# Front of a two-layer graph kernel: products of W a on GpSimd, casts on ScalarE, LayerNorm's scales one step later

## The reference, cut to what matters

```python
h = relu(layernorm(x))
x = x + L0(h, adj, adj, ...)
h = relu(layernorm(x))
x = x + L1(h, adj, W_stack)

# L0
attn_a = sigmoid(concat([adj @ x, x]) @ Wa.T + ba)      # attn_b in the same way
h = x @ W_sa
scores = (h @ a_sa[0, :256])[:, None] + (h @ a_sa[0, 256:])[None, :]
e = where(adj != 0, exp(-leaky_relu(scores, 0.01)), 0)
x_a = (e / (sum(e) + 1e-5)) @ h
x_b = adj @ (x @ W_gcnb) + b_gcnb
return sigmoid(attn_a * x_a + attn_b * x_b)

# L1, twice
Wh, Ws = split(x @ W)
x = leaky_relu((softmax(Wh @ Ws.T) * adj) @ Wh + x)
```

## Time and profile before

| | |
|---|---|
| time, median of 3 runs | 1635.68 us (1634.53 to 1636.81) |
| profiled execution, its own time | 1637.55 us |
| its span in the profile | 1635.7 us |
| granted TensorE clock, mean | 0.994 |
| PE busy | 1566.5 us (96%) |
| DVE busy | 1173.8 us (72%) |
| ACT busy | 1071.0 us (65%) |
| POOL busy | 999.2 us (61%) |
| TensorE busy, first of 40 slices / second | 5 tenths / 9 tenths |

### The profile page before, as it was taken

How to read it: one execution, slowest core, us unless ns; L and a number is a source line. 1 busy time by engine, 2 the same in 40 slices (tenths; PEclk the granted TensorE clock), 3 DMA queues, 4 the chain that set the end, 5 groups by cost and what they waited for, 6 DMA issues and landing times.

```text
span 1635.7 us, 34736 instructions
## 1 busy us (share of the span) xinstructions
PE 1566.5 (96%) x12902; PEld 1541.2 (94%) x12902; DVE 1173.8 (72%) x2165; ACT 1071.0 (65%) x2090; POOL 999.2 (61%) x874
## 2 busy tenths in 40 slices
PE   5999999999999999999999999999999999999984
PEld 5999999999999999999999999999999999999984
DVE  6766766667665677777777778756777777777774
ACT  3579889899984566666666666646666666666653
POOL 2112222222210588888888888838888888888896
PEclk9999999999999999999999999999999999999998
DMA  4124444544430233333333335412333333333332
GB/s 145 40 59 117 123 117 117 146 120 117 123 85 27 55 97 96 98 98 97 98 97 98 98 97 187 156 40 85 102 98 97 99 102 98 98 98 98 98 105 70
DMA packets 88666, 163.36 MB, mean 100 GB/s; under 512 B 9265, under 2 KB 19376, under 8 KB 88240
## 3 DMA queue, kind: packets, MB, share of 16 engines
q1 hardware_dynamic: 60624, 113.41, 23.6%
q0 software_dynamic: 24336, 44.31, 11.0%
q10 hardware_dynamic: 3536, 3.41, 0.6%
HBM read 147.99 MB, written 13.11 MB: 98 GB/s over the span
## 4 chain that ended last, share of the span: by engine, by line
PE 73%; POOL 11%; issue 7%; DVE 4%; ACT 3%; DMA 0%; POOLq 0%; SPq 0%; DVEq 0%; ACTq 0%
PE PS L1128 25%; PE PS L1333 8%; PE PS L1336 7%; PE PS L1335 7%; POOL FR L431 5%; PE PS L1203 5%; PE PS L1200 5%; PE PS L1202 5%; PE PS L1199 5%; PE PS L1201 5%; POOL X L424 5%; DVE AF L953 1%; ACT FR L592 1%; ACT ROW L612 1%; POOL PAB L424 0%
## 5 line engine op out<-in xcount | busy, mean ns | idle before, releaser
L1128 PE MATMUL PS<-FR,RB 128*128 128x256 f32 x4056 | 540.1, 282 | 3.8 <-ACT X L574 1.8
L431 POOL TENSOR_TENSOR FR<-AF,FR 128x512 fp32r<-128x512 f32 x338 | 450.5, 1333 | 134.8 <-ACT FR L592 134.8
L1128 PEld LDWEIGHTS PS<-FR,RB 128*128 128x128 f32 x4056 | 500.7, 188 | 12.3 <-ACT X L574 10.7
L424 POOL TENSOR_TENSOR X<-X,ROW 128x512 f32<-128x512 f32 x294 | 398.9, 1357 | 82.2 <-ACT ROW L602 82.2
L1333 PE MATMUL PS<-FR,RA 128*128 128x256 f32 x1352 | 389.0, 288 | 26.2 <-POOL FR L431 26.1
L1336 PE MATMUL PS<-FR,RA 128*128 128x256 f32 x1352 | 379.7, 281 | 0.0
L1335 PE MATMUL PS<-FR,RA 128*128 128x256 f32 x1352 | 379.0, 280 | 0.0
L953 DVE TENSOR_TENSOR AF<-PS,AJ 128x512 f32<-128x512 f32 x338 | 231.1, 684 | 83.2 <-ACT PS L586 82.1
L1333 PEld LDWEIGHTS PS<-FR,RA 128*128 128x128 f32 x1352 | 254.4, 188 | 37.9 <-POOL FR L431 35.5
L397 POOL DMA_DIRECT2D STGT<-adjt x169 | 90.1, 534 | 294.7 <-PE PS L1203 294.7
L574 ACT ACTIVATE X<-PS 128x512 f32<-128x512 f32 x271 | 161.0, 594 | 158.7 <-DVE AF L926 154.2
(11 more groups left out here) (140 smaller groups left out, 2351.8 us busy)
## 6 DMA issues: line engine op xcount, KB each, us to landing
AJ<-adjt SPq DMA_DIRECT2D x338, 256.0 KB, 2.7
STGT<-adjt POOLq DMA_DIRECT2D x169, 256.0 KB, 3.0
xt_scratch<-ROW SPq DMA_DIRECT2D x12, 512.0 KB, 2.6
RB<-xt_scratch SPq DMA_DIRECT2D x12, 512.0 KB, 4.8
x_scratch<-X ACTq DMA_DIRECT2D x13, 256.0 KB, 2.2
ROW<-x_scratch SPq DMA_DIRECT2D x13, 256.0 KB, 3.1
out<-ROW SPq DMA_DIRECT2D x12, 256.0 KB, 3.3
X<-xt SPq DMA_DIRECT2D x1, 1536.0 KB, 11.5
```

What stands on the lines that cost most here:

```text
L424: nc.gpsimd.tensor_tensor(slot, slot, MB.unsqueeze(1).broadcast_to([P, 2, 256]), ALU.subtract)\
L431: nc.gpsimd.tensor_tensor(LO[g % 2], WA[g % 2], HI[g % 3].bitcast(F32), ALU.subtract)\
L1128: last = nc.tensor.matmul(out, stationary(a, k), moving(b, k), start=(k == 0 and i == 0), stop=(k == K - 1 and i == 2))
```

## The change

The two products of W_sa with the halves of a move from VectorE to GpSimd, between its first and second power, and with them the clearing of the spare columns. The two casts (WSL, and WX for h) move from VectorE to ScalarE, between `transposed_high(0)` and `g_high(0, 0)`; ScalarE waits for the left sum, then for the copied right sum and the clearing. VectorE sums the left product ahead of `scales(1)` and the right one behind `normalise(1)`. In the loop, the scales of a LayerNorm part are issued one step later than its variances, behind `transposed_low` and ahead of `normalise`. New semaphores (`wv_pool`, `wv_zero`, `wsl_hi`, `wh_cast`) carry this.

```diff
--- before.py
+++ after.py
@@ -180,7 +180,11 @@
         ln_pow = sem("ln_pow")
         ln_step = sem("ln_step")
         ln_done = sem("ln_done")
+        wv_pool = sem("wv_pool")
+        wv_zero = sem("wv_zero")
         wv_step = sem("wv_step")
+        wsl_hi = sem("wsl_hi")
+        wh_cast = sem("wh_cast")
         w_ready = sem("w_ready")
 
         hn_done = sem("hn_done")
@@ -403,6 +407,14 @@
 
             pool.wait_ge(half_set, 1)
             inverse_root(0, *LN_PARTS[0])
+            pool.wait_ge(w_in, 16)
+            nc.gpsimd.memset(WRAW0[:, :, GX + D + 3:WC], 0.0).then_inc(wv_zero, 1)
+            pool.wait_ge(row_in, 16)
+            for side in range(2):
+                nc.gpsimd.tensor_tensor(PEB[:, :, 0:D] if side == 0 else PAB[:, :, 0:D],
+                                        WRAW0[:, :, GX:GX + D],
+                                        AROW[:, side * D:(side + 1) * D].unsqueeze(1).broadcast_to([P, K, D]),
+                                        ALU.mult).then_inc(wv_pool, 1)
             inverse_root(1, *LN_PARTS[1])
             for n in range(NSTG):
                 load_unit(n)
@@ -522,6 +534,12 @@
             act.wait_ge(w_in, 16)
             nc.scalar.activation(WX[:, 0, :, 0:GX], WRAW0[:, :, 0:GX], ACT.Copy).then_inc(wg_hi, 1)
             transposed_high(0)
+            act.wait_ge(wv_step, 1)
+            nc.scalar.activation(WSL[:, 0, :, :], WV[:, 0, :].unsqueeze(2).broadcast_to([P, K, P]), ACT.Copy)\
+              .then_inc(wsl_hi, 1)
+            act.wait_ge(wv_step, 3)
+            act.wait_ge(wv_zero, 1)
+            nc.scalar.activation(WX[:, 0, :, GX:WC], WRAW0[:, :, GX:WC], ACT.Copy).then_inc(wh_cast, 1)
             for p in range(PAIRS):
                 if 1 <= p < PAIRS - 1:
                     transposed_high(p + 1)
@@ -844,32 +862,26 @@
             statistics(2, 6)
             variances(1, 2, 6, 2)
             transposed_low(0)
-            dve.wait_ge(row_in, 16)
-            for side in range(2):
-                nc.vector.tensor_tensor(PEB[:, :, 0:D] if side == 0 else PAB[:, :, 0:D],
-                                        WRAW0[:, :, GX:GX + D],
-                                        AROW[:, side * D:(side + 1) * D].unsqueeze(1).broadcast_to([P, K, D]),
-                                        ALU.mult).then_inc(wv_step, 1)
+            dve.wait_ge(wv_pool, 1)
+            nc.vector.reduce_sum(WV[:, 0, :], PEB[:, :, 0:D], AX).then_inc(wv_step, 1)
             scales(1, 2, 6)
             normalise(1)
+            dve.wait_ge(wv_pool, 2)
+            nc.vector.reduce_sum(WV[:, 1, :], PAB[:, :, 0:D], AX).then_inc(wv_step, 1)
             dve.wait_ge(wv_step, 2)
-            nc.vector.reduce_sum(WV[:, 0, :], PEB[:, :, 0:D], AX).then_inc(wv_step, 1)
-            nc.vector.reduce_sum(WV[:, 1, :], PAB[:, :, 0:D], AX).then_inc(wv_step, 1)
-            dve.wait_ge(wv_step, 4)
             nc.vector.tensor_copy(WRAW0[:, :, GX + D + 2:GX + D + 3], WV[:, 1, :].unsqueeze(2)).then_inc(wv_step, 1)
-            nc.vector.memset(WRAW0[:, :, GX + D + 3:WC], 0.0).then_inc(wv_step, 1)
-            nc.vector.tensor_copy(WSL[:, 0, :, :], WV[:, 0, :].unsqueeze(2).broadcast_to([P, K, P]))\
-              .then_inc(wv_step, 1)
-            dve.wait_ge(wv_step, 7)
-            nc.vector.tensor_copy(WX[:, 0, :, GX:WC], WRAW0[:, :, GX:WC]).then_inc(wv_step, 1)
+            dve.wait_ge(wsl_hi, 1)
             nc.vector.tensor_tensor(WSL[:, 1, :, :], WV[:, 0, :].unsqueeze(2).broadcast_to([P, K, P]),
                                     WSL[:, 0, :, :].bitcast(F32), ALU.subtract).then_inc(w_ready, 1)
-            dve.wait_ge(wv_step, 8)
+            dve.wait_ge(wh_cast, 1)
             nc.vector.tensor_tensor(WX[:, 1, :, GX:WC], WRAW0[:, :, GX:WC], WX[:, 0, :, GX:WC].bitcast(F32),
                                     ALU.subtract).then_inc(w_ready, 1)
             for p in range(PAIRS):
                 if 1 <= p < PAIRS - 1:
                     transposed_low(p + 1)
+                if p - 1 in LN_CHAIN:
+                    i = LN_CHAIN[p - 1]
+                    scales(i, *LN_PARTS[i])
                 if 1 <= p < PAIRS - 2:
                     normalise(p + 2)
                 g_low(p, 0)
@@ -892,7 +904,6 @@
                 if p in LN_CHAIN:
                     i = LN_CHAIN[p]
                     variances(i, *LN_PARTS[i], 2 + sum(b <= LN_PARTS[i][1] for a, b in LN_STATS.values()))
-                    scales(i, *LN_PARTS[i])
             mask0(UNITS - 1)
 
             def xt_low(u):
```

## The result

| | before | after |
|---|---|---|
| median | 1637.97 us (6 runs, 1634.53 to 1639.67) | 1632.10 us (6 runs, 1631.00 to 1633.08) |
| profiled execution, own time / span | 1637.55 / 1635.7 | 1631.97 / 1630.2 |
| mean granted clock | 0.994 | 0.996 |

The ratio after to before is 0.9967, 95% interval 0.9954 to 0.9980: 5.9 us by the medians. The change is faster; the upper end of the interval lies on the 0.2% that the prediction took as its border. The kernel before was timed again beside the later experiments: 1637.09 (21 runs), 1637.27 (9) and 1636.77 (21). The three runs shown ahead of the prediction were low ones. The mean granted clock of each run goes with its time. Of the 51 runs timed again, the 21 at 0.996 took 1634.48 to 1636.38 us, and the 30 at 0.993 to 0.995 took 1636.77 to 1640.54.

A forecast was written before the change was run, and what follows sets the result against it. TensorE bounds the kernel after 70 us and waits for VectorE before. 1.38 + 1.13 + 0.48 + 2.5 + 1.4 - 1.45 + 1.45 = 6.9 us gives 1630.6, or 1630.1 from the median; forecast 1630.3, range 1628.2 to 1633.2.

The forecast's parts named there:

- four signs: Forecast wrong if second power starts late, L841 is stretched, 0.50 stands in later windows, or rest does not follow front.
- The weights: Weight preparation in the front: last W subtraction starts at 15.08 instead of 16.46, 1.38 us earlier.
- The ports: SBUF ports shared by VectorE and GpSimd during weight preparation: neither holds the other up; no time charged.
- rival (b): Contention: GpSimd's product starts before L841, pushing the statistics by about 0.6; 1630.9, at most 1632.2; chance 0.10.
- The first h at full clock: First 12 matmuls of h, behind the shortened hole before 17.21: full instead of half clock, 1.13 us.
- The scales: Scales one step later: 0.48 at step 1, 2.5 plus 1.4 clock at step 3, 1.45 at step 6, 1.45 given back.
- The sum of the front: All gains before 70 us, from weights, clock and scales less the new waits: 6.9 us.
- The rest moves with it: After 70 us TensorE is busy almost throughout: a start d us shorter moves all of it up by d.
- The profiled execution against the median: Median 1635.68 is 1.87 below profiled 1637.55; a median run has one of two half-clock losses, so gain lowered by 1.3.
- Rival (a): Clock: first h stays at half (-1.1) or a fall lands at step 4 or 5 (-1.4); 1631.6 to 1632.8; chance 0.22.
- (c): Front: ScalarE's wait or the new hole takes back what steps 1 and 3 win; 1634.3; chance 0.08.
- (d): GpSimd's products run late and delay the second power; from 5.4 us late the front is longer; 1638.8; chance 0.05.

The follow-up runs named there:

- Weights_only: Changed kernel with the scales back at the end of the step that has their variances; median 1635.10 us, ratio to the kernel before 0.9989.
- four_timed: Changed kernel with two more GpSimd products of the same size ahead of the two, into unread scratch; median 1632.79 us, ratio to the kernel before 0.9977.
- casts_back: Changed kernel with both casts on VectorE again, products still on GpSimd; median 1632.58 us, ratio to the kernel before 0.9972.
- seam: Changed kernel, at n = 11 of the second loop high0(12) ahead of exp0(13) and leaky0(14), low0(12) ahead of mask0(13); median 1630.08 us, ratio 0.9958.
- products_behind: Changed kernel, but GpSimd waits for VectorE's subtraction L859 before its first product; 1631.66 us in one run.

## Why the prediction was right

Forecast 1630.3, range 1628.2 to 1633.2; measured 1632.1 on the first chip and 1630.83 on a later one. Time and range came out, and the front did as forecast. But of the four signs by which the prediction said it would be wrong, three showed: L841 was stretched, 0.50 stands in a later window, and the rest did not move with the front in full. Step by step:

- **The weights.** Subtraction forecast at 15.08, measured 15.01; the price of a product, 1.31 from L424, was high: one with nothing beside it takes 1.09. Weights_only confirms the gain at the mark.
- **The ports.** This step failed. The prediction held, from the multiplication at 11.43 beside the power in the earlier trace rows, that neither engine holds the other up. With products in the power's place, they do, for the whole instruction. A power over four elements was no like row for a product over 512. The order of rival (b) came in the first profile, the product first. Instead of the 0.55 to 0.6 it charged it cost nothing: L859 ended at 8.79, and the statistics behind it wait for a load of x until 8.7 anyway. The rival had set the start of the product 0.4 us later. What it did not see is normalise(0): with the row of a landing 0.04 us sooner than in that profile (7.00), as in four_timed (6.96), the product holds that up, and TensorE's first transposes come 0.9 us later. That this costs the changed kernel as much is an extrapolation: four_timed has two more products.
- **The first h at full clock.** It is, in ten of the twelve profiles with the products on GpSimd: 1.65 to 1.74 us. But it is not safe: in one of two profiles of casts_back's code (2.73) and one of two of four_products' (2.67) it ran mostly at half clock. `l(0)` before it, which the prediction did not price, took 1.65 in the first profile against 0.98 in the earlier trace rows, and so filled the 0.29 of hole that had stood behind it.
- **The scales.** 0.48 + 2.5 + 1.4 and the 1.45 at step 6 less the new wait: measured alone 4.66. The new hole before h(4) was forecast at 1.2 and is 0.91, and the one before h(3) at about 0.2 and is 0.19. One reading behind this was incomplete: in the kernel before, half clock followed three holes and not two, as the row below this list shows.
- **The sum of the front.** 6.9 forecast, 6.76 measured. It is no cancelling of errors: by TensorE's start at each point, 2.7 us at the first unit (3.0 forecast), 6.4 behind step 3 (6.9), 5.1 behind step 4 (5.45). The missing 0.3 at the first unit is about the pause between the scale instructions.
- **The rest moves with it.** This step failed too, by 1.47 us. The prediction looked at clock falls in the front only, and took from 45.5 us on having none in one profile that there would be none. The same hole of 1.95 us that is harmless in one execution costs 1.5 in the next.
- **The profiled execution against the median.** It took the profiled one for 1.87 us slower than a median run and lowered the gain by 1.3 for that. Later medians of before, 1636.77 to 1637.97, put 1637.55 in their middle: three runs did not carry that step. It was right that runs differ by stretches of half clock, and wrong on which is the common case, since 30 of the 51 later runs are in the slower group. Here there was luck. From 1635.68 the forecast is a gain of 5.4 us, and the medians give 5.9; but this nearness rests on 1.3 taken off for a wrong reason, in place of the 1.47 that a fall at 106 us takes and that was not foreseen. The base that was too low leaves the forecast 1.8 us low on one chip and 0.5 on the other.

The third stretch of half clock in the kernel before, by its windows:

```profile
29.00:30.00 1.00, 1.00 (x7) 1.00 (x6) 0.56 (x3) 1.00 (x4) 0.00 (x0) 0.50 0.00 0
```

It lies behind the hole of 2.78 and lasts from about 28.3 to 31.7 us. The prediction has no term for it, and none was due: from `l(2)` to the first unit TensorE took 5.17 us before (29.29 to 34.46) and 5.49 at full clock after (26.26 to 31.75), since there it waits for VectorE (0.31 and 0.92). So a fall in this stretch cost nothing, and the one at 106 us, where TensorE is the bound, cost 1.47.

Rival (a) was half right (falls decide 1.5 us, but at 106 us, not at steps 4 and 5), (c) is refuted by both halves, and (d) has the right slope up to the last subtraction in the one profile that tests it, but its point was never near: the products ended 1.07 us ahead of the second power.

## What to carry to other kernels

Where an engine waits a fixed time for another's small result, put behind it nothing that a third engine needs sooner: issuing the transposed low part ahead of the scales, with no work moved to another engine, won 4.7 us of the front alone; the moves between engines won 1.9 to 2.4. When a hole of about 2 us in TensorE's work cannot be closed, halve it: seam won 0.7 us of idle time, and its five times lay within 0.2 us. And compare traces at a fixed mark inside them: three profiles of the changed kernel agree there to 0.04 us, where medians of these kernels need about 2. But look at the length of the first h as well, since two profiles of the same code, one with the first h at half clock, lay 1.0 us apart (casts) and 1.4 (four products).

## What the runs showed of the hardware

- A VectorE instruction with two SBUF inputs and a GpSimd product shut each other out whole: 0.69 became 1.59 us when the product had started first; a product of 1.09 became 1.41 to 1.61 when VectorE had, and ended 0.95 to 0.96 us behind VectorE's instruction each time. A normalisation with one SBUF input seems to be hit too: 1.61 us instead of 0.74 for two, in four_timed alone. The power on GpSimd did not do this to VectorE's multiplication at 11.43 in the earlier trace rows. With products_behind's wait for `wg_ready` both are avoided at no cost to the mark; that was run once only (1631.66).
- Behind the same hole of 1.96 us, in the same code, the granted clock fell to 0.50 for 3 to 4 us in two profiles and not in a third; over all kernels, in six of eleven. It fell behind the holes of 2.05, 2.78 and 2.71 us of the kernel before and not behind its 1.45; the 0.91 to 1.05 left in the changed kernel brought none in three profiles.
- At the start of the program the granted clock reads 1.00 while matmuls of 258 columns take 0.419 us, the length they have at 0.50 (0.420); later, at 1.00, they take 0.28. In four_products and casts_timed no stretch reads under 1.00, yet the first h took 2.67 and 2.73 us. So in these profiles the row of the granted clock does not show the half rate of the first matmuls, and their length does.
